# A deformable-convolution stage: tents and weights by quarters of pixels, three comparisons moved to DVE, and a reordered end

## The chip, the cores and the metric

The kernel runs on one NeuronCore of a Trainium2 chip. The metric is the device time of one execution in microseconds (us); the median of three runs is given for the kernel before. Engine names: PE is the matrix engine (PEld its weight loads), DVE the vector engine, ACT the scalar engine, POOL the GpSimd engine, SP the engine that issues the DMAs.

## What is computed

The whole program is four layers, each a convolution-like block and a feed-forward block, on x of 8 images, 64 channels, 16 x 16 pixels. The change touches one block, the deformable convolution of the second layer. For each image, each of 4 channel groups and each of 9 taps (36 "samples"), a position is predicted per pixel, the image is sampled there with bilinear weights, and the samples are contracted over taps and channels:

```python
offset = conv2d_same(conv2d_same(xd, w1, b1), w2, b2)
py = dy + ky + hh;  px = dx + kx + ww
y0 = floor(py);  x0 = floor(px)
val = gather(y0, x0) * (wy0 * wx0) + gather(y0, x0 + 1) * (wy0 * wx1) \
    + gather(y0 + 1, x0) * (wy1 * wx0) + gather(y0 + 1, x0 + 1) * (wy1 * wx1)
out = relu(einsum('ogck,bgckhw->bohw', wr, val));  x = x + out
```

## The kernel before

`build` writes each of the eight blocks as one program per engine, with semaphores between them and a barrier after each block. The deformable stage stands at L928 to L1261. Its 2048 pixels (8 images of 256) are 16 tiles of 128.

Start of the stage. PE computes the offsets (L1023, L1048) for four quarters of the pixels (`n` in `range(NB)`, two images each). DVE makes positions (L1208), their clamped floor (L1212 to L1214) and a 16-bit linear index `IDX` (L1216) quarter by quarter. PE transposes the indices (L1055), ACT copies them (L1140), SP stores them in `idx_dram` (L988) and, when all four quarters are there, loads them back, one sample a DMA, broadcast to all 128 partitions, into a ring `BC` of 4 (L995). After all quarters DVE subtracts the floor from all positions at once (L1221), ACT makes the two tents `U0` = relu(1 - |frac|) and `U1` = relu(1 - |frac - 1|) in four passes of 128x1152 (L1147, L1148), and DVE multiplies them into the corner weights `WC` in four instructions (L1228), which also divide by GSCALE (4096, the scale of the 16-bit gather source `GX`).

The loop over the 36 samples. A one-hot matrix says which of 256 source pixels an output pixel wants, in two halves of 128 rows (`qh`). DVE's `compare(s)` (L1237) makes half 0 of every sample, and half 1 too where s is a multiple of 3. For the other 24 samples ACT makes half 1 in two passes, `DIST` = |index - q| (L1162) and relu(1 - DIST) (L1165). The one-hots are a ring of 3 (`OH`), so ACT's second pass and the compare wait for gather s - 3. PE's `gather(s)` (L1073) is 64 matmuls that pick the four corners of every pixel. DVE's `weigh(s)` (L1248) multiplies them by `WC` in two instructions into `U` (the tiles SQ and SD in turn). POOL adds the four corners in two instructions (L1008, L1011) into `VAL`. Every 8 samples (a chunk) PE's `contract` transposes `VAL` (L1090, four groups `q` of four transposes, in two PSUM banks in turn), ACT's `evac` copies each group to `VTA` (L1154), and `project` (L1099) multiplies by `wd`. DVE adds relu of it to X (L1261).

Each engine executes its own program in order; the order is written out by hand. DVE's is: compare(0), compare(1), the weights, then per sample compare(s + 1), weigh(s). ACT's has evac(0), (1), (2) after the one-hots of samples 13, 21 and 29, and evac(3), evac(4) at the end. PE's is

```python
for s in range(SAMPLES):
    gather(s)
    if s >= 11 and s % 8 == 3:
        contract(s // 8 - 1)
    if s >= 15 and s % 8 == 7:
        project(s // 8 - 1)
contract(4)
project(3)
project(4)
```

SP waits, ahead of the broadcast of sample s, for both halves of the one-hot of sample s - 4.

## Time and profile before

| | us |
|---|---|
| median of 3 runs | 609.9 (608.07 to 611.87) |
| the profiled execution | 609.04 |
| its span, first to last instruction | 607.3 |
| mean granted TensorE clock in it | 0.963 |
| PE, DVE, ACT, POOL busy over the span | 513.8, 365.2, 293.1, 142.8 |

All durations come from one profiled execution, which took 609.04 us, 1.7 more than its span. A timeline row gives the start in us from the span's start, the length, the engine, the line, the operation, what it wrote and read, how many instructions were merged, and in brackets the idle time before it and what ended that. Merged rows hold instructions that follow one another without a gap. A group's row gives busy time, the mean of one instruction, and the idle time in front of the group's instructions.

### The profile page before, as it was taken

The page shows a single profiled execution, that of the slowest core. Times are in us where ns is not written, and L with a number is a line of the kernel's source. Part 1 is how long each engine was busy: PE and PEld are TensorE (multiplying, and loading weights), DVE is VectorE, ACT ScalarE, POOL GpSimd, SP SyncE. Part 2 cuts the span into 40 slices and gives each one's busy share as a digit, 9 for nine tenths or more (in the row PEclk, how much of TensorE's full clock was granted, in tenths as well). Part 3 has the DMA queues.
Part 4 walks back from the last instruction along what each step waited for, and adds up shares of the span by engine and source line. Part 5 has one row for each costly group of instructions (what it writes and reads, how often), then busy time and mean ns, then how long its engine had stood idle before and what let it go on. Part 6 is the DMA issues. An engine that isn't in the chain of part 4 may idle for free. (4 is left out here: it accounts for less than half of the span.)

```text
span 607.3 us, 11742 instructions
## 1 busy us (share of the span) xinstructions
PE 513.8 (85%) x4973; PEld 263.1 (43%) x4973; DVE 365.2 (60%) x587; ACT 293.1 (48%) x393; POOL 142.8 (24%) x136
## 2 busy tenths in 40 slices
PE   3899989878998996788888788749997898999994
PEld 1334324543224966777687442313323334433231
DVE  2377994673554559878869257561437796633534
ACT  2573225255531159999998356635551102344230
POOL 8070000010011005888878300042002002000000
PEclk9999999998998999899899889868999999999998
DMA  7000000020000035455452000110002000000000
GB/s 251 1 2 2 2 1 1 1 102 0 1 16 16 2 104 206 160 184 195 176 177 74 1 19 0 49 42 0 1 13 101 0 1 1 1 0 1 3 15 17
DMA packets 7988, 29.42 MB, mean 48 GB/s; under 512 B 864, under 2 KB 2176, under 8 KB 7552
## 3 DMA queue, kind: packets, MB, share of 16 engines
q1 hardware_dynamic: 7936, 28.67, 14.1%
q8 instruction: 39, 0.64, 0.4%
q14 instruction: 13, 0.11, 0.1%
HBM read 28.00 MB, written 0.67 MB: 47 GB/s over the span
## 5 line engine op out<-in xcount | busy, mean ns | idle before, releaser
L1073 PE MATMUL PS<-GX,OH 128*128 128x64 f16 x2304 | 73.6, 195 | 19.1 <-DVE OH L1237 9.5
L1073 PEld LDWEIGHTS PS<-GX,OH 128*128 128x128 f16 x2304 | 71.0, 99 | 24.1 <-issue 12.7
L1162 ACT ACTIVATE DIST<-BC,wbuf 128x2048 f16<-128x2048 f16 x24 | 48.0, 2000 | 3.1 <-DMA BC<-idx_dram 1.4
L1969 DVE TENSOR_SCALAR HID<-PS,wbuf 128x512 f32<-128x512 f32 x32 | 23.8, 750 | 41.6 <-PE PS L1862 41.6
L1165 ACT ACTIVATE OH<-DIST 128x2048 f16<-128x2048 f16 x24 | 45.9, 1911 | 0.8
L1237 DVE TENSOR_SCALAR OH<-BC,wbuf 128x2048 f16<-128x2048 f16 x48 | 43.8, 935 | 2.6 <-DMA BC<-idx_dram 2.6
L1008 POOL TENSOR_TENSOR V<-SQ 128x512 f32<-128x512 f32 x18 | 27.9, 1547 | 57.5 <-DVE SQ L1248 56.7
L1908 ACT ACTIVATE HID<-PS,wbuf 128x512 f32<-128x512 f32 x32 | 22.0, 687 | 37.1 <-PE PS L1862 37.1
L692 DVE SCALAR_TENSOR_TENSOR D<-QKVP,wbuf,D 128x1024 f32<-128x1024 f32 x27 | 34.6, 1281 | 7.7 <-ACT D L592 6.9
L181 ACT ACTIVATE SQ<-PS 128x512 f32<-128x512 f32 x16 | 9.6, 597 | 60.9 <-PE PS L153 52.7
L153 PE MATMUL PS<-X,wconst 128*128 128x512 f32 x32 | 19.2, 731 | 22.9 <-DMA wconst<-pack_dram 8.6
L1858 PE MATMUL PS<-Y,wbuf 64*128 64x512 f32 x128 | 36.6, 615 | 2.3 <-DVE HID L1969 2.3
L423 PE MATMUL PS<-T,DG 128*32 128x512 f32 x336 | 37.1, 594 | 0.0
L1011 POOL TENSOR_TENSOR VAL<-V 128x256 f32<-128x256 f32 x36 | 35.9, 997 | 2.8
L1248 DVE TENSOR_TENSOR SQ<-PS,WC 128x512 f32<-128x512 f32 x36 | 23.1, 683 | 14.7 <-PE PS L1073 13.3
L921 DVE TENSOR_TENSOR HS<-PS,HID 128x512 f32<-128x512 f32 x32 | 20.6, 685 | 18.5 <-PE PS L806 18.4
L1870 PE MATMUL PS<-HID,wbuf 128*64 128x512 f32 x128 | 30.8, 604 | 0.0
L1008 POOL TENSOR_TENSOR V<-SD 128x512 f32<-128x512 f32 x18 | 26.7, 1485 | 4.8 <-DVE SD L1248 3.8
L873 ACT ACTIVATE HID<-PS,wbuf 128x512 f32<-128x512 f32 x32 | 20.1, 682 | 13.2 <-PE PS L797 13.1
L1248 DVE TENSOR_TENSOR SD<-PS,WC 128x512 f32<-128x512 f32 x36 | 23.1, 681 | 5.6 <-PE PS L1073 3.3
L1628 DVE TENSOR_TENSOR H2W<-H,WB 128x512 f32<-128x512 f32 x16 | 10.5, 689 | 24.7 <-ACT H L1569 12.5
L592 ACT ACTIVATE D<-PS,wbuf 128x512 f32<-128x512 f32 x12 | 8.3, 689 | 28.6 <-PE PS L423 28.6
(309 smaller groups left out, 931.0 us busy)
## 6 DMA issues: line engine op xcount, KB each, us to landing
BC<-idx_dram SPq DMA_DIRECT2D x36, 512.0 KB, 4.2
wbuf<-pack_dram SPq DMA_DIRECT2D x1, 1913.0 KB, 10.2
wbuf<-pack_dram SPq DMA_DIRECT2D x1, 1656.0 KB, 6.8
wbuf<-pack_dram SPq DMA_DIRECT2D x1, 1494.5 KB, 6.1
wbuf<-pack_dram SPq DMA_DIRECT2D x1, 820.0 KB, 11.7
wbuf<-pack_dram SPq DMA_DIRECT2D x1, 732.0 KB, 4.2
wbuf<-pack_dram SPq DMA_DIRECT2D x1, 602.5 KB, 3.4
X<-x_dram SPq DMA_DIRECT2D x2, 256.0 KB, 4.2
```

Source lines behind the costliest of these rows:

```text
L423: mm = pe.matmul(bank(DBANK[t % 2] + n)[32 * q:32 * q + 32, :], DG[:, (2 * j + hf) * NBLK + i, :], src, start=(i == blocks[0]), stop=(i == ...
L692: ins = dve.scalar_tensor_tensor(out=d, in0=window(QKVP[j], dy, dx), scalar=wt("dw5", j * 25 + 5 * dy + dx, 1), in1=d, op0=ALU.mult, op1=A ...
L1008: after_pool(pool, pool.tensor_tensor(V1[:, :, :, :], U[s % 2][:, :, 0:2, :], U[s % 2][:, :, 2:4, :], ALU.add))
L1011: pool.tensor_tensor(VAL[:, (s // 8) % 2, :, s % 8, :], V1[:, :, 0, :], V1[:, :, 1, :], ALU.add).then_inc(val_ready, 1)
L1073: mm = pe.matmul(o, OH[:, s % NOH, qh, t * P:(t + 1) * P], src, start=(qh == 0 and part == 0), stop=(qh == 1 and part == 1))
L1162: after_act(act, act.activation(DIST[:, :], BC[:, s % NBC, :], ACT.Abs, bias=wt("negq1")))
L1165: act.activation(OH[:, s % NOH, 1, :], DIST[:, :], ACT.Relu, bias=1.0, scale=-1.0).then_inc(scalar_oh, 1)
L1237: ins = dve.tensor_scalar(OH[:, s % NOH, qh, :], BC[:, s % NBC, :], wt("qidx", qh, 1), None, ALU.is_equal)
L1248: ins = dve.tensor_tensor(o, src, w, ALU.mult)
L1858: pe.matmul(bank(2 + (n + bh) % 4), wt("w1_3", e * FH3 + m * P, P, r, r + C), Y[r:r + C, bp * HC:(bp + 1) * HC], start=True, stop=False, t ...
L1870: pe.matmul(bank(bp)[C * bh:C * bh + C, :], wt("w2_3", (2 * e + m) * C, C), HID[:, (n + i) % 8, :], start=(e == 0 and m == 0), stop=False) ...
L1969: dve.tensor_scalar(HID[:, n % 8, :], bank(2 + n % 4), wt("b1_3", 2 * e + m, 1), 0.0, ALU.add, ALU.max).then_inc(hid_in_v, 1)
```

## The change

- Tents and weights by quarters. DVE subtracts the floor for each quarter right behind that quarter's indices. ACT's `tents(n)` makes the tents of quarter n in four passes of 128x288: quarters 0, 1, 2 ahead of its copies of the transposed indices, quarter 3 after its last corner copies. DVE's `corner_weights(n)` is four products of 144 elements a partition: quarters 0 and 1 behind the position work of quarters 1 and 2, quarters 2 and 3 ahead of compare(0).
- The weights are no longer divided by GSCALE; the evacuations of `VTA` are, by their scale.
- Samples 5, 13 and 29 leave ACT (`ON_ACT` has 21 samples): DVE's compare makes both halves.
- The end. contract(3) stands between gather(34) and gather(35) (it stood behind gather(35)), project(3) ahead of contract(4) (it stood behind it). POOL adds samples 0 to 34; DVE makes the two sums of sample 35. contract(4) takes its groups in the order 0, 2, 1, 3; ACT evacuates the first and third, DVE the second and fourth; project(4) waits for each half by itself.

```diff
+            ON_ACT = [s for s in range(SAMPLES) if s % 3 and s % 8 != 5]
             def scalars(s):
-                return s - s // 3
+                return sum(k <= s for k in ON_ACT)
+            LAST = (0, 2, 1, 3)
...
@@ gpsimd
-                for s in range(SAMPLES):
+                for s in range(SAMPLES - 1):
@@ tensor, contract(ch)
-                    pe.wait_ge(val_ready, 8 * ch + ns)
-                    for q in range(4):
-                        n = 4 * ch + q
-                        if n >= 2:
+                    pe.wait_ge(val_ready, min(8 * ch + ns, SAMPLES - 1))
+                    if ch == 4:
+                        pe.wait_ge(last_val, 1)
+                    for j, q in enumerate(LAST if ch == 4 else range(4)):
+                        n = 4 * ch + j
+                        if n == 19:
+                            pe.wait_ge(vt_dve, 1)
+                        elif n >= 2:
                             pe.wait_ge(vt_in, n - 1)
@@ tensor, project(ch)
-                    pe.wait_ge(vt_in, 4 * ch + 4)
+                    if ch < 4:
+                        pe.wait_ge(vt_in, 4 * ch + 4)
                     for bp in range(2):
+                        if ch == 4:
+                            pe.wait_ge(vt_in, 17 + bp)
+                            pe.wait_ge(vt_dve, 1 + bp)
@@ tensor, the loop
-                    if s >= 11 and s % 8 == 3:
+                    if s in (11, 19, 27, 34):
                         contract(s // 8 - 1)
...
+                project(3)
                 contract(4)
-                project(3)
                 project(4)
@@ scalar
+                def tents(n):
+                    act.wait_ge(frac_ready, n + 1)
+                    for u, at in ((U0, 0.0), (U1, -1.0)):
+                        o = tiles4(u[:, :, :], n)
+                        after_act(act, act.activation(o, tiles4(PY[:, :, :], n), ACT.Abs, bias=at if at == 0.0 else wt("minus1")))
+                        act.activation(o, o, ACT.Relu, bias=1.0, scale=-1.0).then_inc(tents_ready, 1)
                 for n in range(4):
                     corners(n)
+                for n in range(3):
+                    tents(n)
...
-                act.wait_ge(frac_ready, 1)
-                for u, at in ((U0, 0.0), (U1, -1.0)):
-                    after_act(act, act.activation(u[:, :, :], PY[:, :, :], ACT.Abs, bias=at if at == 0.0 else wt("minus1")))
-                    act.activation(u[:, :, :], u[:, :, :], ACT.Relu, bias=1.0, scale=-1.0).then_inc(tents_ready, 1)
+                tents(3)
@@ scalar, evac(ch)
-                    for q in range(4):
-                        act.wait_ge(vt_ps, 4 * ch + q + 1)
+                    for j, q in enumerate(LAST if ch == 4 else range(4)):
+                        if ch == 4 and j % 2:
+                            continue
+                        act.wait_ge(vt_ps, 4 * ch + j + 1)
...
-                    if s % 3:
+                    if s in ON_ACT:
@@ vector
+                def corner_weights(n):
+                    dve.wait_ge(tents_ready, 2 * n + 2)
+                    at = 4 * (n % 2) + 2 * (n // 2)
+                    for k in range(4):
+                        wy = tiles4((U0, U1)[k // 2][:, :, :], n)[:, :, :, 0:36]
+                        wx = tiles4((U0, U1)[k % 2][:, :, :], n)[:, :, :, 36:72]
+                        o = WC[:, :, :, k].rearrange("p s (h t) -> p h t s", h=2)[:, :, at:at + 2, :]
+                        ins = dve.tensor_tensor(o, wy, wx, ALU.mult)
+                    ins.then_inc(wc_ready, 1)
...
                     ins.then_inc(idx_ready, 1)
+                    dve.tensor_tensor(py, py, base, ALU.subtract).then_inc(frac_ready, 1)
+                    if n in (1, 2):
+                        corner_weights(n - 1)
                 for n in range(4, 2 * NB):
                     corners(n)
-                dve.tensor_tensor(PY[:, :, :], PY[:, :, :], BASE[:, :, :], ALU.subtract).then_inc(frac_ready, 1)
+                corner_weights(2)
+                corner_weights(3)
...
-                    for qh in range(1 if s % 3 else 2):
+                    for qh in range(1 if s in ON_ACT else 2):
...
-                corner_weights()
+                dve.wait_ge(wc_ready, NB)
...
+                last = SAMPLES - 1
...
+                after(dve, dve.tensor_tensor(sums, U[last % 2][:, :, 0:2, :], U[last % 2][:, :, 2:4, :], ALU.add))
+                dve.tensor_tensor(VAL[:, (last // 8) % 2, :, last % 8, :], sums[:, :, 0, :], sums[:, :, 1, :], ALU.add).then_inc(last_val, 1)
+                for j in (1, 3):
+                    q = LAST[j]
+                    dve.wait_ge(vt_ps, 16 + j + 1)
+                    dve.tensor_scalar(VTA[0:64, 0, q * 512:(q + 1) * 512], bank(j % 2)[0:64, :], 1.0 / GSCALE, None, ALU.mult).then_inc(vt_dve, 1)
```

On ACT, at the start of the loop: U0 and U1 are the tents, PY the fractions, IDXT the transposed indices, GX the gather source, DIST and OH the two passes of a one-hot. Before:

```order
L1133 ACTIVATE GX<-PS 128x512 x4
L1140 ACTIVATE IDXT<-PS 36x2x256 x4
L1133 ACTIVATE GX<-PS 128x512 x4
L1147 ACTIVATE U0<-PY 128x1152
L1148 ACTIVATE U0<-U0 128x1152
L1147 ACTIVATE U1<-PY,wbuf1 128x1152
L1148 ACTIVATE U1<-U1 128x1152
L1162 ACTIVATE DIST<-BC,wbuf1 128x2048
L1165 ACTIVATE OH<-DIST 128x2048
```

The same place after, from the last of the three early quarters on:

```order
L1152 ACTIVATE U0<-PY 128x2x144
L1153 ACTIVATE U0<-U0 128x2x144
L1152 ACTIVATE U1<-PY,wbuf1 128x2x144
L1153 ACTIVATE U1<-U1 128x2x144
L1161 ACTIVATE IDXT<-PS 36x2x256 x4
L1145 ACTIVATE GX<-PS 128x512 x4
L1152 ACTIVATE U0<-PY 128x2x144
L1153 ACTIVATE U0<-U0 128x2x144
L1152 ACTIVATE U1<-PY,wbuf1 128x2x144
L1153 ACTIVATE U1<-U1 128x2x144
L1183 ACTIVATE DIST<-BC,wbuf1 128x2048
```

Four wide passes behind the corner copies became four narrow ones there and twelve ahead of the copies of indices.

On PE, the end of the stage, from the gathers of samples 28 to 31 on (L1073 are gathers, L1090 transposes, L1099 the projection; in the new numbering L1077, L1098, L1111). Before:

```order
L1073 MATMUL PS<-GX,OH 128x64 x256
L1099 MATMUL PS<-VTA,wbuf 64x512 x4
L1073 MATMUL PS<-GX,OH 128x64 x256
L1090 MATMUL PS<-wconst,VAL 128x128 x16
L1090 MATMUL PS<-wconst,VAL 64x128 x16
L1099 MATMUL PS<-VTA,wbuf 64x512 x8
```

After:

```order
L1111 MATMUL PS<-VTA,wbuf 64x512 x4
L1077 MATMUL PS<-GX,OH 128x64 x192
L1098 MATMUL PS<-wconst,VAL 128x128 x16
L1077 MATMUL PS<-GX,OH 128x64 x64
L1111 MATMUL PS<-VTA,wbuf 64x512 x4
L1098 MATMUL PS<-wconst,VAL 64x128 x16
L1111 MATMUL PS<-VTA,wbuf 64x512 x4
```

The 16 transposes of chunk 3 moved ahead of the last gather's 64 matmuls, and four of the last eight projections ahead of the last chunk's transposes.

On DVE, the end of the stage (SQ and SD are U; PY is reused for the first sum). Before:

```order
L1248 TENSOR_TENSOR SD<-PS,WC 128x512 x2
L1237 TENSOR_SCALAR OH<-BC,wbuf 128x2048
L1248 TENSOR_TENSOR SQ<-PS,WC 128x512 x2
L1248 TENSOR_TENSOR SD<-PS,WC 128x512 x2
L1261 SCALAR_TENSOR_TENSOR X<-PS,X 128x512 x2
```

After:

```order
L1263 TENSOR_SCALAR OH<-BC,wbuf 128x2048
L1274 TENSOR_TENSOR SQ<-PS,WC 128x512 x2
L1274 TENSOR_TENSOR SD<-PS,WC 128x512 x2
L1287 TENSOR_TENSOR PY<-SD 128x512
L1288 TENSOR_TENSOR VAL<-PY 128x16x16
L1292 TENSOR_SCALAR VTA<-PS 64x512 x2
L1296 SCALAR_TENSOR_TENSOR X<-PS,X 128x512 x2
```

Two sums and two evacuations stand between the last weighing and the last adds.

## Rows read from the trace of the kernel before

**Rows 1.** The page, busy us of each engine, share, instructions

```profile
PE 513.8 (85%) x4973; PEld 263.1 (43%) x4973; DVE 365.2 (60%) x587; ACT 293.1 (48%) x393; POOL 142.8 (24%) x136
```

**Rows 2.** Two stretches: busy us by engine (instructions), granted clock, DMA

```profile
240.00:335.00 95.00, 77.72 (x2129) 69.94 (x2125) 76.02 (x106) 88.63 (x55) 80.41 (x64) 0.96 0.48 162
...
340.00:342.00 2.00, 1.59 (x8) 0.61 0.00 0
```

**Rows 3.** The page, costliest groups: busy us, mean ns, idle before them

```profile
L1162 ACT ACTIVATE DIST<-BC,wbuf 128x2048 f16<-128x2048 f16 x24 | 48.0, 2000 | 3.1 <-DMA BC<-idx_dram 1.4
...
L1165 ACT ACTIVATE OH<-DIST 128x2048 f16<-128x2048 f16 x24 | 45.9, 1911 | 0.8
...
L1237 DVE TENSOR_SCALAR OH<-BC,wbuf 128x2048 f16<-128x2048 f16 x48 | 43.8, 935 | 2.6 <-DMA BC<-idx_dram 2.6
...
L1248 DVE TENSOR_TENSOR SQ<-PS,WC 128x512 f32<-128x512 f32 x36 | 23.1, 683 | 14.7 <-PE PS L1073 13.3
...
L1248 DVE TENSOR_TENSOR SD<-PS,WC 128x512 f32<-128x512 f32 x36 | 23.1, 681 | 5.6 <-PE PS L1073 3.3
```

**Rows 4.** Timeline of ACT, start of the loop: start us, us, instruction

```profile
216.81 1.55 ACT L1140 ACTIVATE IDXT<-PS 36x512 f16<-36x512 f16 x3 [16.48 <-PE PS L1055]
...
228.49 1.99 ACT L1162 ACTIVATE DIST<-BC,wbuf 128x2048 f16<-128x2048 f16 x1
```

**Rows 5.** Timeline of DVE, start of the loop

```profile
212.05 0.46 DVE L1208 TENSOR_TENSOR PY<-PS,POS 128x288 f32<-128x288 f32 x1 [2.53 <-PE PS L1048]
...
226.44 2.08 DVE L1237 TENSOR_SCALAR OH<-BC,wbuf 128x2048 f16<-128x2048 f16 x3 [2.60 <-DMA BC<-idx_dram]
...
228.61 4.64 DVE L1228 SCALAR_TENSOR_TENSOR WC<-U 128x576 f32<-128x576 f32 x4
...
236.35 1.89 DVE L1237 TENSOR_SCALAR OH<-BC,wbuf 128x2048 f16<-128x2048 f16 x2
```

**Rows 6.** Timeline of ACT: evacuations (L1154) and last one-hot (L1165)

```profile
265.19 1.07 ACT L1154 ACTIVATE VTA<-PS 128x512 f32<-128x512 f32 x2
...
287.91 1.09 ACT L1154 ACTIVATE VTA<-PS 128x512 f32<-128x512 f32 x2 [0.32 <-PE PS L1090]
...
314.27 1.07 ACT L1154 ACTIVATE VTA<-PS 128x512 f32<-128x512 f32 x2
...
331.36 1.91 ACT L1165 ACTIVATE OH<-DIST 128x2048 f16<-128x2048 f16 x1
...
335.90 1.09 ACT L1154 ACTIVATE VTA<-PS 128x512 f32<-128x512 f32 x2 [2.63 <-PE PS L1090]
```

**Rows 7.** Lines: count, duration ns min/median/max; broadcasts to landing

```profile
L1237 DVE TENSOR_SCALAR OH<-BC,wbuf x46: 734/744/1775, 227.8 to 332.5; 128x2048 f16<-128x2048 f16 x46
...
L1011 POOL TENSOR_TENSOR VAL<-V x36: 728/1063/1256, 236.4 to 339.6; 128x256 f32<-128x256 f32 x36
...
L1008 POOL TENSOR_TENSOR V<-SQ x18: 1259/1606/1697, 234.7 to 336.1; 128x512 f32<-128x512 f32 x18
...
DMA to landing us min/median/max: 3.3/4.2/6.8
```

**Rows 8.** Timeline of PE, last gathers and end of the stage

```profile
331.49 3.91 PE L1073 MATMUL PS<-GX,OH 128*128 128x64 f16 x128 [0.25 <-DVE OH L1237]
...
335.23 1.07 PE L1090 MATMUL PS<-wconst,VAL 128*128 128x128 f32 x8
...
336.55 1.15 PE L1090 MATMUL PS<-wconst,VAL 128*128 128x128 f32 x8 [0.25 <-ACT VTA L1154]
...
340.41 3.61 PE L1090 MATMUL PS<-wconst,VAL 128*64 128x128 f32 x16 [2.71 <-POOL VAL L1011]
```

**Rows 9.** Timelines of DVE (first two) and POOL, end of the stage

```profile
336.16 1.29 DVE L1248 TENSOR_TENSOR SD<-PS,WC 128x512 f32<-128x512 f32 x2 [0.88 <-POOL VAL L1011]
...
347.80 0.69 DVE L1261 SCALAR_TENSOR_TENSOR X<-PS,X 128x512 f32<-128x512 f32 x1 [0.17 <-PE PS L1099]
...
339.62 0.73 POOL L1011 TENSOR_TENSOR VAL<-V 128x256 f32<-128x256 f32 x1
```

More of the change, by code:

```diff
@@ L968, in build @@
                 "val_ready", "vt_ps", "vt_in", "dc_ps", "xs_ready"))
+            vt_dve, wc_ready, last_val = sem("s3_vt_dve"), sem("s3_wc_ready"), sem("s3_last_val")
             bc_in = [sem(f"bc_in{i}") for i in range(NBC)]
@@ L1089, in contract @@
                             src = VAL[:, ch % 2, t, 0:ns, :].rearrange("p s c -> p (s c)")
-                            mm = pe.transpose(bank(q % 2)[0:rows, i * P:(i + 1) * P], src, wt("ident"))
+                            mm = pe.transpose(bank(j % 2)[0:rows, i * P:(i + 1) * P], src, wt("ident"))
                         mm.then_inc(vt_ps, 1)
@@ L1218, in _ @@
                     ins.then_inc(idx_ready, 1)
+                    dve.tensor_tensor(py, py, base, ALU.subtract).then_inc(frac_ready, 1)
+                    if n in (1, 2):
+                        corner_weights(n - 1)
                 for n in range(4, 2 * NB):
                     corners(n)
-                dve.tensor_tensor(PY[:, :, :], PY[:, :, :], BASE[:, :, :], ALU.subtract).then_inc(frac_ready, 1)
-                def corner_weights():
-                    dve.wait_ge(tents_ready, 2)
-                    for k in range(4):
-                        wy = (U0, U1)[k // 2][:, :, 0:36].rearrange("p t s -> p s t")
-                        wx = (U0, U1)[k % 2][:, :, 36:72].rearrange("p t s -> p s t")
-                        ins = dve.scalar_tensor_tensor(out=WC[:, :, :, k], in0=wy, scalar=1.0 / GSCALE, in1=wx,
-                                                       op0=ALU.mult, op1=ALU.mult)
-                    after(dve, ins)
+                corner_weights(2)
+                corner_weights(3)
                 def compare(s):
@@ L1257, in _ @@
                     weigh(s)
+                last = SAMPLES - 1
+                sums = PY[:, :, :].rearrange("p t k -> p (t k)")[:, 0:TILES * 2 * CG].rearrange("p (t k c) -> p t k c", k=2, c=CG)
+                dve.wait_ge(u_ready, last + 1)
+                after(dve, dve.tensor_tensor(sums, U[last % 2][:, :, 0:2, :], U[last % 2][:, :, 2:4, :], ALU.add))
[4 more added lines that the diff above has]
+                    dve.tensor_scalar(VTA[0:64, 0, q * 512:(q + 1) * 512], bank(j % 2)[0:64, :], 1.0 / GSCALE, None, ALU.mult).then_inc(vt_dve, 1)
                 for bp in range(2):
```

3 lines of the change are left out of this document (2 added, 1 removed).

## The prediction

> **What bounds the kernel now.** I read four views in this order: the page's busy line, the stretches of the deformable stage, the engines' timelines at the stage's seams, and the page's costliest groups.
>
> The busy line [rows 1] makes TensorE look like the bound (85%), but that is a mean over eight stages. The change touches one stage, so only that stage's rows count. In its main stretch, 240 to 335 us [rows 2], ACT is busy 88.63 of 95 us, POOL 80.4, PE 77.7, DVE 76.0. The groups say why [rows 3]: 24 samples have half their one-hot made by two ACT passes of 2.00 and 1.91 us. With the issue between them that is 4.03 us each, 96.7 us in all. DVE makes the same 128x2048 half in one compare of 0.744 us (median). The stage has 36 samples, and PE needs 2.0 us for each (3.91 us for two gathers [rows 8]). So from ACT's first pass (228.49) to its last (331.36 + 1.91 = 333.27 [rows 4, 6]) ACT sets the time: 104.8 us, of which 96.7 are one-hots and some 7.2 three evacuations.
>
> The ends of the stage are different. Ahead of 226.44 us everything waits for the first broadcast of indices. After 333.27 us comes a serial tail [rows 8, 9]: gather of sample 35, a weighing that waits for POOL, two sums on POOL until 339.62 + 0.73 = 340.35, transposes, evacuations, projection, last add ending at 347.80 + 0.69 = 348.49. That tail is 15.2 us long and nothing lies beside it.
>
> **Part 1: tents and weights by quarters.** ACT's four full tents go; they ended at 228.5, since its first pass stands behind them without idle time. Twelve of the sixteen small tents (288 wide against 1152) now run in ACT's idle time before 216.81 (16.48 us idle in that row [rows 4]), four after its last corner copies. The third quarter's four should be over at about 216.2 (its subtraction ends near 214.4, four passes of some 0.4), ahead of the copy of transposed indices at 216.81. DVE's four weight products, 4.64 us between the compares and the first weighing, become sixteen of a quarter size. Eight go into the idle time before its position work (2.53 us idle in the row at 212.05 [rows 5]), eight into the stretch before the first broadcast lands. Size of one: a 576-wide product took 1.16 us, so a 144-wide one is an estimated 0.35, bounds 0.29 (a quarter) and 1.16 (no smaller). Four of them are 1.4 us, inside the 2.53 us gap. At the upper bound four would be 4.6 us, and the set ahead of the last quarter's position work would push the first broadcast by 2.1. I take 0.35 because these rows scale with width (the 288-wide addition at 212.05 took 0.46 us).
>
> What this gives: the second broadcast had landed by the third compare, at most 227.8 (three compares from 226.44 without idle time [rows 5]). ACT starts there and not at 228.49: 0.7 us, at most 2.1 if the data were there at 226.4. DVE's 4.64 us give nothing by themselves: gather 2 waits for ACT's second one-hot, not for a weighing.
>
> **Part 2: samples 5, 13 and 29 to DVE.** ACT loses 3 x 4.03 = 12.1 us, DVE gains three compares: 0.744 us each when free, 0.91 by the group (43.8 / 48), 1.78 at most. DVE had 20.3 us idle in front of its weighings [rows 3], so 2.7 us have room. But ACT does not keep 12.1 us, because it meets PE at each evacuation. I work by the stretches between ACT's evacuations [rows 6].
>
> First stretch, 228.49 to 265.19 (36.7 us, nine one-hots). Now seven: 227.8 + 28.2 = 256.0. Sample 7 follows sample 4 at once and wants its broadcast at 239.9. Its buffer (a ring of four) is refilled after compare 3, which ended at 238.24 [rows 5] and comes at most 1.3 us earlier; with 4.2 us (median) to landing [rows 7] that is 241.3, a new wait of 1.5. Sample 10, behind DVE's 9, the same with 0.6. That makes 258.1. The evacuation used to come after one-hot 13 and found its data ready. Now it comes after one-hot 11 and must wait for gather 11 (2.0) and the first transposes (0.67 from 335.23 to 335.90, as in the row of the third evacuated chunk [rows 6, 8]) with 0.1 of semaphores: 260.9. I add 0.3 for DVE's double compare in front of gather 9: 261.2. Gain 4.0 with the 0.7 of part 1; bounds 0.7 and 8.8 (two whole one-hots and the start).
>
> Second stretch, 265.19 to 287.91: five one-hots before and after, nothing.
>
> Third stretch, 287.91 to 314.27 (26.4 us, six one-hots). Now five. Evacuations 2.3, four one-hots 16.1 to the end of one-hot 26, gathers 26 and 27 4.1, transposes 0.7: 23.2, and I give compare 27 up to 0.7 of lateness: 23.9. Gain 2.5; bounds 0 and 4.0. The rest up to the last one-hot has four one-hots in both.
>
> At the price of these compares there is a port in common. The rows show POOL's sum taking 0.73 us at least and 1.26 at most, its first sum 1.26 and 1.70, and a DVE compare 0.734 to 1.775 [rows 7]. The Trainium skill (SBUF — State Buffer, section Who interferes with whom) says that whichever of the two starts first holds the shared pair for its whole instruction and the other blocks fully. By it an added compare would cost up to 0.744 + 1.26 = 2.0 and three 6.0; by the group's mean three cost 2.7. The spread of these rows agrees with the rule, and its consequence is the first rival.
>
> **Part 3: the end.** Times from E, the end of the last one-hot (before 333.27). Gather 34 ends at E + 0.15. The transposes of chunk 3 now stand before gather 35 and take 2.47 us (335.23 to 337.70 [rows 8]): E + 2.6. This is a cost: they ran before in PE's idle time. Gather 35 to E + 4.6, weighing 1.29 and 0.1 to E + 6.0. In the cover of this POOL finishes sample 34. The two last sums on DVE: 0.69 (a 512-wide one of 1.29 for two) and an estimated 0.4 for 256 columns, to E + 7.1. The last transposes start at E + 7.2; before, 340.41, E + 7.14. So here the reordering and the sums on DVE cancel.
>
> From there: before, 8.08 us to 348.49, with the transposes at a granted clock of 0.61 [rows 2], after 2.71 us of idle PE. Now the projection of chunk 3 (1.9: two projections lie between 344.02 and the last add at 347.80 [rows 8, 9]) stands in that gap, so idle is some 0.7 us and I take the full clock. First transposes 0.5, first evacuation over at 1.3, DVE's at 1.9, third group at 1.35 to 1.85, fourth at 1.95 to 2.45, DVE's second evacuation 2.6 to 3.3, projection of the first half from 2.5 to 3.5, of the second to 4.4, last add to 5.4. Gain 2.7, less 0.1 for the later start: 2.6. Bounds: 1.0 (clock low again, each group 0.9 instead of 0.5) and 3.2.
>
> The Trainium skill, same page and section, also says that a DVE instruction with two SBUF inputs contends with POOL's reads. The last sums are of that kind. By it they would wait for POOL's sums of sample 34, up to 1.26; since those end while gather 35 still runs, the sum is the same, and no row of this profile shows such a pair.
>
> **The sum.** 4.0 + 2.5 + 2.6 = 9.1 us. The profiled execution took 609.04 (span 607.3 and 1.7 around it): 599.9. The median shown is 0.9 above it: 600.8.
>
> **The rivals.**
> 1. DVE and POOL take the place of ACT (gain under 1%). Each added compare stands behind another compare of the same pair of samples and costs its longest, 1.78, on the path: 5.3 of the 6.5 us of parts 1 and 2. 1.2 + 2.6 = 3.8: 606.1. For it: POOL is busy 80.4 of 95 us and the compares' spread is wide. Against: DVE is idle 20.3 us, and a median compare takes 0.744. Chance 0.18.
> 2. ACT keeps everything: 12.1 + 0.7 + 2.6 = 15.4: 594.5. It needs gathers 11 and 27 and broadcasts 7 and 10 not to be late. Against it is the order of ACT's evacuations. Chance 0.08.
> 3. The end gives nothing: chunk 3's transposes in front of gather 35 meet a low clock, gather 35 takes 2.6 and the last transposes 3.6 again. 6.5 - 1.5 = 5.0: 604.9. Chance 0.05.
> 4. Slower: DVE becomes the bound of the whole loop. DVE's 111.0 us from 226.44 to 337.45 are 43.8 of compares, 46.2 of weighings, 4.6 of products and 20.3 idle, less 3.9 of overlap. If the idle time stays and compares stretch beside a denser POOL to midway between 0.744 and 1.775 (1.26), 51 x 1.26 + 46.2 + 20.3 - 3.9 = 126.9: 15.9 more, less 2.6: 623.2. It decides from a mean compare of 1.00 us on (51 x 1.00 = 111.0 + 2.6 - 46.2 - 20.3 + 3.9), against 0.91 now. Against it: the idle time is time behind ACT's one-hots and should shrink. Chance 0.04.
>
> **How the numbers follow.** Forecast 0.65, rivals as above. A measurement of this kernel tells about 1% (6.1 us) from no change. Nearly all of the forecast's cases and rival 2 are beyond it: 0.63 + 0.08 = 0.71 faster. Rivals 1 and 3 and the weak end of the forecast: 0.25 same. Rival 4: 0.04 slower. The forecast's own range is 598 to 604. With rival 1 above, and below half of the way to rival 2, the range is 596.5 to 606.
>
> **What would show it.** ACT's first pass starts at 227.0 to 227.9. ACT waits for a DMA about 1.5 us before its one-hot of sample 7. First evacuations start near 261.2, 284, 308 and the last one-hot ends near 326.8. Gather 35 starts 2.5 us after gather 34 ends; the last transposes start some 7.2 us after the last one-hot and the stage's last add ends 5.4 us later at a granted clock near 1. Mean of the 51 compares 0.90 to 0.97. The forecast is wrong if DVE's idle time before the weighings stays near 20 us, if the sixteen small products push the first compare past 226.44, or if other stages move by more than 0.5 us.

## The result and the profile after

| | before | after the change |
|---|---|---|
| median | 610.05 us (4 runs, 608.07 to 611.87) | 601.86 us (4 runs, 600.62 to 602.63) |
| ratio to before, 95% interval | | 0.9861 (0.9824 to 0.9898) |
| profiled execution: span, mean granted clock | 607.3 us, 0.963 | 599.2 us, 0.973 |
| stage: first compare's start to last add's end | 226.44 to 348.49, 122.05 us | 227.60 to 342.69, 115.09 us |

The forecast was 600.8. Of the 8.1 us between the two spans, 6.96 lie in the stage as measured here; outside it there are 1.2 us more ahead of the first compare and 2.3 less behind the last add. The 1.2 us are not the small products' doing, though they stand there: PE's second convolution of the stage, ahead of all of them, already began at 199.61 in place of 198.43, and from it to the first compare it is 27.99 us (28.01 before). All times below that start with "+" count from the first compare, so that the two executions can be laid on each other. "Length of the stage" is the last row of the table. Some executions are more than 1.5% slower than the fastest of their kernel, and the ratios, here and below, leave them out; of proj_22 these were four in six, so its ratio says little.

ACT's side, from its timeline after the change: start, length, line, operation and in brackets the idle time before it. L1183 and L1186 are the two passes of a one-hot, L1174 the evacuations.

```profile
228.83 2.00 ACT L1183 ACTIVATE DIST<-BC,wbuf 128x2048 f16<-128x2048 f16 x1 [4.42 <-DMA BC<-idx_dram]
...
243.31 2.00 ACT L1183 ACTIVATE DIST<-BC,wbuf 128x2048 f16<-128x2048 f16 x1 [2.46 <-DMA BC<-idx_dram]
...
262.81 1.09 ACT L1174 ACTIVATE VTA<-PS 128x512 f32<-128x512 f32 x2 [3.44 <-PE PS L1098]
...
286.09 1.09 ACT L1174 ACTIVATE VTA<-PS 128x512 f32<-128x512 f32 x2 [0.86 <-PE PS L1098]
...
311.52 1.09 ACT L1174 ACTIVATE VTA<-PS 128x512 f32<-128x512 f32 x2 [3.02 <-PE PS L1098]
...
328.53 1.91 ACT L1186 ACTIVATE OH<-DIST 128x2048 f16<-128x2048 f16 x1
```

These answer to [rows 4, 6]. The first pass stands at +1.23 (+2.05 before). The row at 243.31 is the new wait for the broadcast of sample 7, 2.46 us. The evacuations stand at +35.21, +58.49 and +83.92 (before +38.75, +61.47, +87.83), each now with idle time in front, in which ACT waits for PE's transposes: 3.44, 0.86 and 3.02 us in place of 0, 0.32 and 0. The last one-hot ends at 330.44, +102.84, against +106.83. So ACT gave up 12 us of work and finished 4.0 us earlier.

DVE at the start of the loop, its timeline (L1232 are the small weight products):

```profile
210.98 1.19 DVE L1232 TENSOR_TENSOR WC<-U 128x144 f32<-128x144 f32 x4
...
213.22 0.46 DVE L1239 TENSOR_TENSOR PY<-PS,POS 128x288 f32<-128x288 f32 x1 [1.05 <-PE PS L1052]
...
223.68 2.16 DVE L1232 TENSOR_TENSOR WC<-U 128x144 f32<-128x144 f32 x8
...
227.60 2.08 DVE L1263 TENSOR_SCALAR OH<-BC,wbuf 128x2048 f16<-128x2048 f16 x3 [1.76 <-DMA BC<-idx_dram]
```

Four products take 1.19 us and fit into the gap; 1.05 us of it are left at 213.22 (2.53 before, [rows 5]). That row stands 1.17 us later than before, as the whole execution does there. The last eight end at 225.84, and DVE still waits 1.76 us for the broadcast.

The page's groups of DVE (busy us, mean ns, idle in front):

```profile
L1263 DVE TENSOR_SCALAR OH<-BC,wbuf 128x2048 f16<-128x2048 f16 x51 | 47.1, 949 | 1.8 <-DMA BC<-idx_dram 1.8
...
L1274 DVE TENSOR_TENSOR SQ<-PS,WC 128x512 f32<-128x512 f32 x36 | 23.2, 684 | 11.6 <-PE PS L1077 9.5
...
L1274 DVE TENSOR_TENSOR SD<-PS,WC 128x512 f32<-128x512 f32 x36 | 23.1, 682 | 7.7 <-PE PS L1077 5.0
```

Against [rows 3]: three more compares at nearly the same mean (949 and 935 ns), and still 19.3 us idle in front of the weighings (20.3 before).

The third stretch, PE's timeline: gather 23, projection, gathers 24 and 25, 26, 27.

```profile
296.49 2.83 PE L1077 MATMUL PS<-GX,OH 128*128 128x64 f16 x64 [2.01 <-issue]
...
299.25 2.70 PE L1111 MATMUL PS<-VTA,wbuf 128*64 128x512 f32 x8
...
301.88 3.91 PE L1077 MATMUL PS<-GX,OH 128*128 128x64 f16 x128
...
305.96 2.04 PE L1077 MATMUL PS<-GX,OH 128*128 128x64 f16 x64 [0.18 <-DVE OH L1263]
...
308.97 2.04 PE L1077 MATMUL PS<-GX,OH 128*128 128x64 f16 x64 [0.97 <-DVE OH L1263]
```

And DVE's in the same place: weighing of sample 25, compare of 27 in two halves.

```profile
305.82 1.29 DVE L1274 TENSOR_TENSOR SD<-PS,WC 128x512 f32<-128x512 f32 x2
...
307.03 1.89 DVE L1263 TENSOR_SCALAR OH<-BC,wbuf 128x2048 f16<-128x2048 f16 x2
```

PE waited 2.01 us for ACT's one-hot 23, then ran gather 23 in 2.83 us and the projection in 2.70 (2.03 and 1.94 at the full clock). From 297.5 to 300.5 us the granted clock was 0.50, the lower of its two levels (1.2 of 2.4 GHz); from 302 to 306 it was 1.00 again. Everything up to gather 27 stands in a row behind that. The kernel before ran the same two as low, in its own PE timeline:

```profile
298.31 2.63 PE L1073 MATMUL PS<-GX,OH 128*128 128x64 f16 x64 [2.01 <-issue]
...
300.87 2.92 PE L1099 MATMUL PS<-VTA,wbuf 128*64 128x512 f32 x8
```

There it cost nothing, as the experiments show; here it does.

The tail, PE's timeline and then DVE's, answering to [rows 8, 9]:

```profile
330.63 1.07 PE L1098 MATMUL PS<-wconst,VAL 128*128 128x128 f32 x8
...
332.93 2.03 PE L1077 MATMUL PS<-GX,OH 128*128 128x64 f16 x64
...
334.89 1.94 PE L1111 MATMUL PS<-VTA,wbuf 128*64 128x512 f32 x8
...
337.58 1.03 PE L1098 MATMUL PS<-wconst,VAL 128*64 128x128 f32 x8 [0.75 <-issue]
...
338.86 1.16 PE L1098 MATMUL PS<-wconst,VAL 128*64 128x128 f32 x8 [0.24 <-ACT VTA L1174]
```

```profile
335.00 1.29 DVE L1274 TENSOR_TENSOR SD<-PS,WC 128x512 f32<-128x512 f32 x2 [2.46 <-PE PS L1077]
...
336.32 0.69 DVE L1287 TENSOR_TENSOR PY<-SD 128x512 f32<-128x512 f32 x1
...
337.05 0.43 DVE L1288 TENSOR_TENSOR VAL<-PY 128x256 f32<-128x256 f32 x1
...
342.00 0.69 DVE L1296 SCALAR_TENSOR_TENSOR X<-PS,X 128x512 f32<-128x512 f32 x1 [0.23 <-PE PS L1111]
```

From the last one-hot's end E = 330.44: chunk 3's transposes over at E + 2.66, gather 35 at E + 4.52, weighing at E + 5.85, sums at E + 7.04, last transposes start at E + 7.14, last add ends at E + 12.25 (15.22 before).

### The profile page after: what moved, and what is told of

Its sections match the earlier page's. It is cut to its first block and busy times, and to the rows that moved or that the text cites. A ratio compares the mean times of both kernels' runs of the same rounds, so it can differ in the third digit from the quotient of the medians.

```text
span 599.2 us, 11757 instructions
## 1 busy us (share of the span) xinstructions
PE 509.2 (85%) x4969; PEld 261.3 (44%) x4973; DVE 371.0 (62%) x609; ACT 282.8 (47%) x397; POOL 142.2 (24%) x134
## 5 line engine op out<-in xcount | busy, mean ns | idle before, releaser
L1077 PE MATMUL PS<-GX,OH 128*128 128x64 f16 x2304 | 72.6, 194 | 18.9 <-DVE OH L1263 12.7
L1077 PEld LDWEIGHTS PS<-GX,OH 128*128 128x128 f16 x2304 | 69.9, 98 | 23.9 <-DVE OH L1263 15.0
L1263 DVE TENSOR_SCALAR OH<-BC,wbuf 128x2048 f16<-128x2048 f16 x51 | 47.1, 949 | 1.8 <-DMA BC<-idx_dram 1.8
L1183 ACT ACTIVATE DIST<-BC,wbuf 128x2048 f16<-128x2048 f16 x21 | 42.0, 2001 | 8.9 <-DMA BC<-idx_dram 7.5
L1186 ACT ACTIVATE OH<-DIST 128x2048 f16<-128x2048 f16 x21 | 40.1, 1911 | 0.7
L1274 DVE TENSOR_TENSOR SD<-PS,WC 128x512 f32<-128x512 f32 x36 | 23.1, 682 | 7.7 <-PE PS L1077 5.0
```

Of the source, the lines that this page charges most:

```text
L1077: mm = pe.matmul(o, OH[:, s % NOH, qh, t * P:(t + 1) * P], src, start=(qh == 0 and part == 0), stop=(qh == 1 and part == 1))
L1183: after_act(act, act.activation(DIST[:, :], BC[:, s % NBC, :], ACT.Abs, bias=wt("negq1")))
L1186: act.activation(OH[:, s % NOH, 1, :], DIST[:, :], ACT.Relu, bias=1.0, scale=-1.0).then_inc(scalar_oh, 1)
L1263: ins = dve.tensor_scalar(OH[:, s % NOH, qh, :], BC[:, s % NBC, :], wt("qidx", qh, 1), None, ALU.is_equal)
L1274: ins = dve.tensor_tensor(o, src, w, ALU.mult)
```

## The experiments

Each kernel was profiled once and timed in several rounds beside the kernel before. "Length" is the length of the stage in the profile, "tail" the time from the end of the last one-hot to the end of the last add. A stretch is, as in the prediction, the time between the starts of two of ACT's evacuations; the first begins with ACT's first pass. "Low clock" sums what PE's gathers, transposes and projections took in this stage beyond their full-clock lengths (3.9 us for a pair of gathers, 1.9 for a projection of both halves).

| kernel | length, us | last one-hot ends | tail | low clock, us | ratio to before (95%) |
|---|---|---|---|---|---|
| before | 122.05 | +106.83 | 15.22 | 4.9 | |
| the change | 115.09 | +102.84 | 12.25 | 1.6 | 0.9861 (0.9824 to 0.9898) |
| p1_only | 123.11 | +107.86 | 15.25 | 7.4 | 0.9980 (0.9952 to 1.0008) |
| p2_only | 121.24 | +104.17 | 17.07 | 4.6 | 0.9974 (0.9946 to 1.0002) |
| p3_only | 118.40 | +106.97 | 11.43 | 0 | 0.9890 (0.9849 to 0.9930) |
| no_p1 | 119.82 | +107.53 | 12.29 | 6.0 | 0.9941 (0.9915 to 0.9967) |
| no_p2 | 120.08 | +108.03 | 12.05 | 6.3 | 0.9946 (0.9922 to 0.9971) |
| c3_late | 115.14 | +103.01 | 12.13 | 1.5 | 0.9844 (0.9800 to 0.9888) |
| pool_sums | 116.26 | +102.84 | 13.42 | 1.6 | 0.9847 (0.9819 to 0.9875) |
| ring5 | 115.26 | +102.46 | 12.80 | 1.6 | 0.9900 (0.9854 to 0.9946) |
| proj_22 | 114.22 | +101.78 | 12.44 | 1.5 | 0.9849 (0.9794 to 0.9904) |
| after_busy | 113.66 | +101.28 | 12.38 | 0 | 0.9912 (0.9880 to 0.9944) |
| proj_busy | 114.47 | +102.19 | 12.28 | 0 | 0.9858 (0.9805 to 0.9911) |
| p1_busy | 122.39 | +106.98 | 15.41 | 3.3 | 0.9994 (0.9968 to 1.0021) |

A length is that of one execution, with the low clock that it happened to meet: the column "low clock" differs by up to 7.4 us, more than most of the differences in length. So two lengths are compared below together with that column.

### The parts alone

p1_only is the kernel before with the change's `tents(n)`, `corner_weights(n)`, the fractions by quarters and the scale moved to the evacuations; p3_only has the change's `contract`, `project`, `evac` and the end of POOL's and DVE's programs:

```diff
 p1_only
+                for n in range(3):
+                    tents(n)
+                    dve.tensor_tensor(py, py, base, ALU.subtract).then_inc(frac_ready, 1)
+                    if n in (1, 2):
+                        corner_weights(n - 1)
 p2_only
+            ON_ACT = [s for s in range(SAMPLES) if s % 3 and s % 8 != 5]
 p3_only
-                for s in range(SAMPLES):
+                for s in range(SAMPLES - 1):
+                    if s in (11, 19, 27, 34):
+                project(3)
                 contract(4)
-                project(3)
                 project(4)
```

> The kernel before with the tents and weights by quarters alone. Length of the stage = first compare's start to last add's end (before 122.05 us, after the change 115.09). Theory (ACT sets the loop's time, so only ACT's earlier start counts): ACT starts 0.8 us earlier against the first compare, stage 121.2 to 121.4, whole kernel 0.7 to 0.9 us faster. Rival (DVE's 4.64 us of weights were on the path): stage 117.5. Rival 2 (the small passes delay the index chain): first compare later by 0.5 us or more.

Length 123.11: neither theory. ACT did start 0.8 us earlier (+1.27), and four small products fitted. But PE's timeline has three stretches at the low clock that the kernel before did not have:

```profile
236.60 5.44 PE L1077 MATMUL PS<-GX,OH 128*128 128x64 f16 x128 [1.97 <-issue]
...
257.35 5.33 PE L1077 MATMUL PS<-GX,OH 128*128 128x64 f16 x128 [2.58 <-DVE OH L1253]
...
283.84 5.45 PE L1077 MATMUL PS<-GX,OH 128*128 128x64 f16 x128 [1.85 <-DVE OH L1253]
```

Each follows 1.85 to 2.58 us of idle time and makes its gathers 1.4 to 1.5 us longer. The kernel before had one that is missing here (its gathers 7 and 8). The third of the rows, gathers 18 and 19, is the one that shows in the length: the second evacuation now waits 1.87 us (0.32 before) and the second stretch takes 24.26 us in place of 22.72. Rival 2 is out: the first compare came at 227.24, 0.8 us later, but only 27.89 us behind the start of PE's second convolution (28.01 before). Timed it was 1.2 us faster (0.998), inside its interval of no change.

> The kernel before with samples 5, 13 and 29 on DVE alone. Theory (ACT keeps what PE's order leaves it): the last one-hot ends 3.3 us earlier against the first compare (4.0 in the change with part 1 in it), the tail is as before, 15.2 us, or a little longer if POOL lags: stage 118.5 to 119.2. Rival (all of ACT's 12.1 us are kept): stage 110. Rival 2 (DVE and POOL absorb it): stage 121 to 122.

The last one-hot came 2.7 us earlier (3.3 expected), but the stage only 0.8. After evacuation 2 PE set the time, not ACT, which then waited 4.88 us for chunk 3's transposes. PE's timeline shows why, two pairs of gathers at the low clock, and the projections at the end too (4.97 us, 3.80 before). Between them gather 23, low in the kernel before, ran at the full one (the second row), which matters below:

```profile
281.99 5.45 PE L1077 MATMUL PS<-GX,OH 128*128 128x64 f16 x128 [1.84 <-DVE OH L1249]
...
298.35 2.03 PE L1077 MATMUL PS<-GX,OH 128*128 128x64 f16 x64 [2.01 <-issue]
...
319.19 5.45 PE L1077 MATMUL PS<-GX,OH 128*128 128x64 f16 x128 [1.85 <-DVE OH L1249]
```

The length, 121.24, lies in rival 2's range. But DVE's compares had a mean of 950 ns, as in the change (949), and the two slow pairs alone are 3.1 us: what absorbed the gain was PE's clock.

> The kernel before with the new end alone. Theory: the last one-hot as before, the tail 12.2 to 12.6 us in place of 15.2: stage 119.0 to 119.5. Rival (the new order of the end only pays because ACT and POOL come earlier): tail 14.5 or more, stage 121.3 or more.

As expected and a little more. The tail is 11.43 us. The last transposes and the projection (2.02 us) ran at the full clock:

```profile
340.35 1.03 PE L1098 MATMUL PS<-wconst,VAL 128*64 128x128 f32 x8 [0.74 <-issue]
```

That was no accident of one execution: in all ten profiles with the new end they ran so, and in all four with the old end some of the last transposes or projections ran low.

The other way round, one part taken out of the change:

```diff
 no_p2
-            ON_ACT = [s for s in range(SAMPLES) if s % 3 and s % 8 != 5]
+            ON_ACT = [s for s in range(SAMPLES) if s % 3]
 no_p1
-                for n in range(3):
-                    tents(n)
-                dve.wait_ge(wc_ready, NB)
+                corner_weights()
```

> The changed kernel with samples 5, 13 and 29 back on ACT: the parts 1 and 3 without 2. Theory: the last one-hot 3 to 4 us later against the first compare, tail 12.2, stage 118.0 to 119.0; timed, 3 to 4 us slower than the change. Rival (PE's low clock and DVE take back what ACT gives up, so part 2 is worth little: 1.6 us when made alone): stage 116.0 to 117.0.

Neither: 120.08, and the last one-hot 5.2 us later. The 5.0 us more than the change (the medians, 606.96 and 601.86, say 5.1) are more than part 2 gave alone, but this profile also has 4.7 us more of low clock, so they aren't part 2's worth. Two triples of gathers that take 6.1 us at the full clock took 7.5, of which this is one:

```profile
239.22 7.53 PE L1077 MATMUL PS<-GX,OH 128*128 128x64 f16 x192 [1.96 <-issue]
```

no_p1 has the wide tents again, and the weights behind compare(1).

> The changed kernel with the tents and weights as before the change: parts 2 and 3 without 1. Theory (part 1 gives its 0.8 us of ACT's start once part 2 is there): ACT's first pass 2.0 to 2.4 us after the first compare (1.23 in the change), first evacuation 0.8 later, stage 115.7 to 116.3 plus 1.5 for each more low-clock stretch of PE. Rival (part 1 is a loss, as its stage of 123.1 alone and 120.1 with part 3 against 118.4 of part 3 alone say): stage 113.5 to 115.0.

119.82, with three more low-clock stretches than the change and 4.4 us more of low clock in them. The theory's line with its surcharge of 1.5 for each was 120.2 to 120.8, a little above; the rival's was 113.5 to 115.0 and falls. The first evacuation came 2.57 us later and not 0.8, since two of the three stretches lie ahead of it. ACT's start went from +1.23 to +2.49, PE idled 2.98 us in front of gather 1, and

```profile
233.50 3.44 PE L1077 MATMUL PS<-GX,OH 128*128 128x64 f16 x64 [2.98 <-ACT OH L1186]
...
246.68 7.53 PE L1077 MATMUL PS<-GX,OH 128*128 128x64 f16 x192 [2.11 <-DVE OH L1259]
```

### The clock: dummies in PE's idle time

```diff
                 for s in range(SAMPLES):
+                    if s in (2, 9, 18, 23):
+                        if s > 12:
+                            pe.wait_ge(vt_in, 4 * ((s - 12) // 8 + 1))
+                        keep_busy(pe, 0, 5)
                     gather(s)
```

> Part 1 alone (p1_only), with five dummy matmuls on PE (1.1 us) in the idle time before gathers 2, 9, 18 and 23, where PE had been idle 1.8 to 2.6 us and then ran at the low clock. Theory (part 1 alone lengthened the stage by 1.1 us because PE fell to its low clock in three more places, 1.35 to 1.47 us each): the granted clock stays at 1.00 behind these places, the stage goes from 123.1 to 118.5 to 121.2. Rival (the low clock was hidden behind ACT and the length has another cause): 122.5 to 123.5.

At the four places the clock stayed:

```profile
236.75 3.89 PE L1077 MATMUL PS<-GX,OH 128*128 128x64 f16 x128 [0.89 <-issue]
...
283.12 3.91 PE L1077 MATMUL PS<-GX,OH 128*128 128x64 f16 x128 [0.77 <-DVE OH L1257]
```

The second evacuation came at +60.11 in place of +62.56, 2.45 us earlier. So the stretches were the cause up to there. The third stretch took 26.36 us, as in p1_only, so the 2.45 us were still there at the third evacuation. At the last one-hot only 0.9 were left, and the stage was 122.39, between the two expectations. PE's and then ACT's timeline of p1_busy show where they went:

```profile
314.53 1.54 PE L1094 MATMUL PS<-wconst,VAL 128*128 128x128 f32 x8 [2.73 <-ACT VTA L1168]
...
315.86 5.12 PE L1077 MATMUL PS<-GX,OH 128*128 128x64 f16 x128
```

```profile
319.21 1.91 ACT L1180 ACTIVATE OH<-DIST 128x2048 f16<-128x2048 f16 x1 [0.62 <-PE PS L1077]
...
326.43 2.00 ACT L1177 ACTIVATE DIST<-BC,wbuf 128x2048 f16<-128x2048 f16 x1 [1.27 <-DMA BC<-idx_dram]
```

PE, now ahead, waited 2.73 us for ACT's evacuation (1.13 in p1_only), and the second half of the transposes and gathers 28 and 29 ran low (the granted clock was 0.50 from 316 to 318 us). ACT then took 0.39 us longer over its evacuation, waited 0.6 us for gather 28, which frees a one-hot, and 1.27 us in place of 0.67 for a broadcast: together the 1.57 us. The low clock had moved to the next place where PE idled, and there it was not hidden. Timed, the dummies gained nothing clear (0.9994 against 0.9980).

> The changed kernel with five dummy matmuls on PE (1.1 us) in its idle time before gathers 2, 18, 23 and 30. Theory (the low clock in gather 23 and the projection behind it holds up gather 27 in the third stretch): these take 2.03 and 1.94 us again, third stretch 25.43 to 24.0 to 24.5, stage 113.5 to 114.2. Rival (DVE's compares and ACT end last there): third stretch 25.2 or more, stage 115 or more.

Held, and the third stretch came out even a little below the line. Gather 23 and the projection took their full-clock times, the third stretch 23.87 us in place of 25.43:

```profile
297.98 2.03 PE L1077 MATMUL PS<-GX,OH 128*128 128x64 f16 x64 [0.93 <-issue]
...
299.94 1.94 PE L1111 MATMUL PS<-VTA,wbuf 128*64 128x512 f32 x8
```

With the clock gone from it, what stands in the third stretch is DVE in series with PE: compare 27 waits behind the weighing of 25, which waits for gather 25. Length 113.66, the shortest of all. But the timed median, 603.92, is no better than the change's. In the profiled execution the rest of the program was 5.6 us longer than in the change's (603.4 - 113.66 against 599.2 - 115.09), in code that is the same; behind the last add the mean granted clock was 0.94 there and 0.96 in the change's. Whether the dummies have a part in that isn't shown.

The third stretch can be compared over twelve of the fourteen profiles (the two left moved the projection). Its length, us, by what ACT has to do and by how gather 23 ran:

| | gather 23 low | gather 23 at the full clock |
|---|---|---|
| six one-hots on ACT | before 26.36, p1_only 26.36, no_p2 26.35 | p3_only 26.36, p1_busy 26.36 |
| five one-hots on ACT | the change 25.43, c3_late 25.40, pool_sums 25.45, ring5 25.44, no_p1 25.44 | p2_only 23.87, after_busy 23.87 |

With six, ACT sets the length and the low clock is hidden. With five it costs 1.56 us, and p2_only shows this without a single dummy. Four of the five kernels in the lower left have the change's order up to there, and all four ran gather 23 low, so the change's 25.43 isn't the bad luck of its one profile.

### The third stretch without dummies

```diff
-                    if s >= 15 and s % 8 == 7:
+                    if s in (15, 22, 31):
                         project(s // 8 - 1)
```

> The changed kernel with the projection of chunk 1 behind gather 22 in place of behind gather 23. There PE was idle 2.0 us before gather 23 (waiting for ACT), and gather 23 and the projection then ran at the low clock, 2.83 + 2.70 us in place of 2.03 + 1.94. Theory (PE's chain projection 1, gathers 24 to 27, not ACT, ends last in the third stretch): the projection fills the idle time, the clock stays, gather 27 starts 2 to 3.5 us earlier as far as DVE's compare 27 allows, ACT's third evacuation starts 22.9 to 24.2 us after its second (25.43 in the change), stage 113.0 to 114.3. Rival (DVE's compare 27 or POOL ends last there): 25.0 or more, stage 114.8 to 115.4.

The third stretch took 24.42 us, between theory and rival; the stage, 114.22, lies in the theory's range. Gather 23 and the projection kept the clock, but the idle time moved to gather 26 and the low clock with it:

```profile
297.32 1.94 PE L1111 MATMUL PS<-VTA,wbuf 128*64 128x512 f32 x8
...
307.48 5.44 PE L1077 MATMUL PS<-GX,OH 128*128 128x64 f16 x128 [1.96 <-issue]
```

> The changed kernel with the projection of chunk 1 behind gather 22 and five dummy matmuls on PE ahead of gathers 2, 18, 26 and 30, where it was idle 1.7 to 2.0 us (with the projection moved, the idle time had gone from gather 23 to gather 26, and the low clock with it, 1.46 us). Theory (in the third stretch PE's chain ends last, its low clock included): no low-clock stretch, third stretch 22.9 to 23.6 us (24.42 with the projection moved alone, 25.43 in the change), stage 112.0 to 113.2. Rival (with the clock kept it is ACT's and DVE's chain that ends last, as with dummies alone: third stretch 23.87, stage 113.66): 23.8 or more, stage 113.5 to 114.5. Either way the other stages' clock moves whole-kernel times by more than this.

No low clock, yet the third stretch took 24.34 us. The last matmul of gather 27 stood alone behind 1.21 us in which PE waited for nothing that the profile shows:

```profile
303.42 3.86 PE L1077 MATMUL PS<-GX,OH 128*128 128x64 f16 x127 [0.88 <-issue]
...
308.49 0.19 PE L1077 MATMUL PS<-GX,OH 128*128 128x64 f16 x1 [1.21 <-issue]
```

Both numbers, 24.34 and the stage's 114.47, lie in the rival's ranges. Without that pause the stretch would have been some 23.1 (an estimate), in the theory's range; but the pause is there, so this is open. Pauses of 1.1 to 1.2 us in the middle of a gather are also in the profiles of the kernel before (1.24 us from 249.39 on), p1_only and p1_busy, at other places. Timed, 0.9858: no different from the change.

### The ring and the end

```diff
-            NBC = 4
+            NBC = 5
```

> The changed kernel with five buffers in the ring of broadcasts in place of four. Theory (a new wait on the ring in the first stretch, 2.46 us ahead of the one-hot of sample 7, hidden in part by DVE's chain up to gather 11, since ACT then waited 3.44 us for the transposes): ACT's wait for DMA goes, its wait for the transposes grows by as much, stage 114.6 to 115.3. Rival (the ring holds up the stretch): first evacuation 1 to 2.5 us earlier against the first compare (35.21 in the change), stage 112.8 to 114.0.

The theory held in the main: the wait at sample 7 is gone, ACT's wait for the transposes grew from 3.44 to 5.20, the first evacuation stands at +34.76 against +35.21, and the second, +58.65 against +58.49, has nothing of that left.

```profile
260.62 1.08 ACT L1174 ACTIVATE VTA<-PS 128x512 f32<-128x512 f32 x2 [5.20 <-PE PS L1098]
```

```diff
-                    if s in (11, 19, 27, 34):
+                    if s in (11, 19, 27, 35):
                         contract(s // 8 - 1)
```

> The changed kernel with the transposes of chunk 3 back behind gather 35. Theory (they cost 2.5 us in front of gather 35 and saved nothing but idle time of PE): gather 35 starts 2.5 us earlier, the weighing of sample 35 about 1.7 earlier (then POOL is last), the last transposes 0 to 1.5 us earlier, stage 113.6 to 115.1. Rival (the port shared by DVE and POOL: both inputs of DVE's last sums are in SBUF and POOL still sums sample 34): the first last sum starts or ends later by up to 1.26 us, stage 115 to 115.8.

The last weighing starts 1.6 us earlier (+105.79 against +107.40), the last transposes at +110.00 against +109.98: nothing. The length, 115.14 against 115.09, falls just inside the rival's line, but not by the rival's reason, as the rows below show. PE, with chunk 3's transposes and the projection now behind gather 35, is the last to be ready. This is also the one kernel where DVE's last sums and POOL's of sample 34 overlap. DVE:

```profile
333.30 0.69 DVE L1287 TENSOR_TENSOR PY<-SD 128x512 f32<-128x512 f32 x1
...
334.03 0.84 DVE L1288 TENSOR_TENSOR VAL<-PY 128x256 f32<-128x256 f32 x1
```

POOL:

```profile
333.30 1.29 POOL L1015 TENSOR_TENSOR VAL<-V 128x256 f32<-128x256 f32 x1
```

DVE's second sum took 0.84 us (0.43 in the change) and POOL's 1.29 (0.74). The Trainium skill (SBUF — State Buffer, section Who interferes with whom) has a DVE instruction with two SBUF inputs contend with POOL's reads; this trace agrees, with 0.41 and 0.55 us, and here it cost the stage nothing. In the change itself POOL ended sample 34 at 335.47, before the sums began.

pool_sums gives sample 35's two sums back to POOL:

```diff
-                for s in range(SAMPLES - 1):
+                for s in range(SAMPLES):
...
-                    if ch == 4:
-                        pe.wait_ge(last_val, 1)
```

> The changed kernel with sample 35's two sums back on POOL, all else of the new end kept. POOL is done with sample 34 before the last weighing ends, so it starts at once. Theory (DVE's sums gain only POOL's longer instructions): 1.25 + 0.73 and their gaps in place of 0.69 + 0.43, the last transposes 0.9 to 1.1 us later after the weighing, stage 115.9 to 116.2. Rival (POOL lags at the end as before the change, 1 to 2 us): stage 117 or more.

Length 116.26, 1.17 more, and the last transposes 3.55 us after the weighing's start in place of 2.58. POOL was idle and began at once:

```profile
337.88 1.25 POOL L1012 TENSOR_TENSOR V<-SD 128x512 f32<-128x512 f32 x1 [0.95 <-DVE SD L1272]
...
339.21 0.73 POOL L1015 TENSOR_TENSOR VAL<-V 128x256 f32<-128x256 f32 x1
```

### The same at an equal clock

Executions of one kernel differ by up to 9 us, and the mean granted clock of an execution goes with its time: the kernel before took 606.06 us at 0.974 and 613.17 at 0.952. A least-squares fit over 172 timed executions (one level for each kernel, one slope for all) gives 2.8 us (+-0.5) for each 0.01 of mean clock, with 1.5 us left over. Levels against the kernel before, at an equal clock:

```
kernel        us at equal clock    95%
the change        -6.3           +-1.6
p1_only           -1.5           +-1.0
p2_only           -2.1           +-0.9
p3_only           -2.4           +-1.4
no_p1             -4.5           +-0.9
no_p2             -3.9           +-0.9
c3_late           -6.6           +-1.3
after_busy        -5.7           +-1.2
p1_busy           -0.7           +-0.9
```

At an equal clock the three parts add up, within these intervals: 1.5 + 2.1 + 2.4 = 6.0 against 6.3. Two of them: 2.1 + 2.4 = 4.5 (no_p1: 4.5) and 1.5 + 2.4 = 3.9 (no_p2: 3.9). The mean clock of the change's executions was 0.970, that of the kernel before 0.962: 2.1 us more, 8.4 in all. The correction takes away what a kernel itself does to the clock, so 6.3 is what the order of the work gives and not the whole of what the change gives. Whether the 2.1 us are the change's doing (fewer idle stretches of PE) or the luck of four executions isn't settled; both profiles' 3.3 us less of low clock in the stage speak for the first in part.

## Why the prediction was right

By its own steps:

- The bound. ACT set the loop's time before. For it speak p3_only, where the last one-hot did not move (+106.97), and the third stretch, 26.35 or 26.36 us in all five kernels with six one-hots, whatever PE's clock was. It isn't ACT alone everywhere: in the first stretch p1_only took 37.03 us and p1_busy 36.15, in the second 24.26 and 22.72.
- Part 1, ACT's start: 0.7 forecast, 0.82 measured. The 0.35 us for a small product was 0.30 (1.19 for four). That DVE's weights give nothing fits p1_only, whose stage wasn't shorter, but no run moved them alone. What was missed is that an earlier start changes where PE idles, and with it where it ran at the low clock (p1_only, no_p1).
- Part 2, first stretch: 4.0 with part 1, measured 3.5 (+38.75 to +35.21). The wait for broadcast 7 was 2.46 and not 1.5, that for 10 did not come; ring5 showed that the first mattered for 0.45 us at most: DVE's compares ahead of gathers 9 and 11 ended last. So the step named the wrong wait and had nearly the right sum.
- Part 2, second stretch: nothing forecast, 0.56 lost (22.72 to 23.28). ACT had more time than PE: PE waited 1.85 us for DVE's compare ahead of gather 18, and ACT 0.86 us for the transposes. Kernels whose first evacuation came earlier (+34.72 in after_busy, +34.76 in ring5) had the second at +58.6 all the same.
- Part 2, third stretch: 2.5 forecast, 0.93 measured (26.36 to 25.43). This is the term that was mis-sized. The step let gather 26 start as one-hot 26 was ready, which takes the full clock for granted. At the full clock it was right: 23.9 forecast, 23.87 in p2_only and in after_busy. In the change PE's low clock in gather 23 and the projection made gather 26 start 1.5 us later, and that is the whole miss, 1.56. The trace before has the same two rows low.
- Part 3: 2.6 forecast, 2.97 measured, with every step inside 0.3 us. The full clock that it took for the last transposes stood in all ten profiles with the new end. That the reordering of chunk 3 gives nothing was confirmed by c3_late, that DVE's sums are worth 1.0 to 1.2 by pool_sums.
- The sum: 9.1 forecast, 6.96 in the stage. The median came within 1.1 us of the forecast since 1.1 us more came from the rest of the program, where the prediction had allowed 0.5. That part of the agreement is luck: behind the last add, where the 2.3 us less lie, the mean granted clock was 0.96 in place of 0.95, and nothing in the working speaks of it. With the stage's 6.96 us alone the median would have been some 602.9, still in the range.
- The signs. Three that were to show the forecast wrong came up. The first compare came past 226.44, but the small products had not pushed it. Other stages moved by more than 0.5 us. DVE's idle time stayed near 20 us (19.3), and this sign was badly chosen: up to the last weighing DVE's span shrank by 2.3 us and its work by 1.3 (3.3 us of compares more, 4.6 of products less), so the idle time could hardly shrink, whoever set the pace.
- The rivals. POOL and DVE did not take ACT's place as a whole (compares 949 ns), and no compare mean near 1.00 us came up in the change (the highest of all kernels, in no_p1, was 988 ns). ACT keeping everything was far off. That the end gives nothing fell with p3_only.

## What to carry to other kernels

When work leaves the engine that sets a loop's time, follow the next meeting point (here each evacuation behind PE's transposes), not the sum of the work removed: of 12.1 us taken off ACT 3.2 were kept. Look in the trace before for steps at the slower of the two clock levels, also where they are hidden: when the engine that hid them has less to do, they stand on the path (1.56 us here). And when one idle time of PE is filled, look where the next one is. Compare changes of 1% by the stage's own length from a fixed event, or at an equal mean clock, since whole-kernel times here moved by 2.8 us for each 0.01 of clock.
